# Split of the routed experts' tables in a decoder layer: halves shared by two engines, or whole tables, one engine each

## The chip, the cores and the metric

The kernel runs on one core of one Trainium2 chip. The metric is the device time of one execution in microseconds (us), the median of several runs. A core has five engines that work side by side, each from its own queue of instructions in order: TensorE (PE in the profile; its weight loads are shown apart as PEld), VectorE (DVE), ScalarE (ACT), GpSimd (Pool) and SyncE (SP), which here only starts transfers (DMAs). They wait for one another on semaphores.

## The reference, cut to what matters

One decoder layer over x of 4 x 512 rows of 256 numbers: a Mamba block, then a cross attention, then a mixture of experts, with a layer norm after each. Only the last part is touched:

```
shared = sum over i of _ffn(xf, sw1[i], sw2[i], sw3[i])           # 2 shared experts, all 2048 rows
logits = xf @ router_w.T + expert_bias                            # 8 routed experts
rw, sel = top_k(logits, 2);  rw = softmax(rw)                     # each row goes to 2 of the 8
out = sum over e of combine[:, e] * _ffn(xf, w1[e], w2[e], w3[e])
_ffn(x, w1, w2, w3) = (silu(x @ w1.T) * (x @ w3.T)) @ w2.T        # 256 -> 512 -> 256
```

## The kernel before, in words

The function `experts` runs in three stages. First the first shared expert over all rows (`hidden` and `down`, n = 0 to 3), beside which VectorE sorts the rows by expert. Then the routed experts: the rows, 128 at a time, fill 39 slots (`SLOTS`), each slot with rows of one expert (`owner`). Then the second shared expert (n = 4 to 7), while Pool gathers the slots' results back. The change is in the middle stage and at its two borders.

A product in float32 is made of three: the high part of x by the high part of w, the low part of x by the high part of w, and the high part of x by the low part of w. The high part is a copy rounded to the format fp32r, the low part is the number less its high part. All eight experts' tables lie in on-chip memory (`wall`, per expert three tables of 128 partitions x 1024 columns). Table 0 (w1) and table 1 (w3) of a slot's expert are split anew for each slot, into `wh[0]`, `wl[0]`, `wh[1]`, `wl[1]`; these have one buffer each.

What the engines do for slot j, in the order of their queues:

- TensorE, in the loop near L2400: `turn_x(j+1)` (L2271, two transposes that turn the next slot's rows; they wait until the rows have landed), a read of the slot's owner into a register (`value_load`), `hidden_chosen(j)` (L2289: for part 0 and part 1, that is table 0 and 1, six products: two with x high and w high, two with x low and w high, two with x high and w low), `turn_g(j-1)` (L2300, four transposes) and `down_chosen(j-2)` (L2308). The end of part 0 releases `first_used`, the end of part 1 `h_done`.
- ScalarE, `split_parts(j+1)` (L1925): as soon as `first_used` says that slot j has used table 0, it copies slot j+1's table 0 to `wh[0]`; after `h_done`, table 1 to `wh[1]`. Before the change each copy is two instructions of 512 columns, each of which raises `part_high` by 1. Then `activate(j)` (L1885) and `read_g(j-1)` (L1901).
- VectorE: `read_x(j+1)` (L2065, L2067), the gate of slot j-1 (L2045), `read_y(j-3)` (L2073), then `split_low(j+1, i)` for both tables (L2087): columns 0 to 511 of `wl[i]`.
- Pool: `split_low(j+1, i)` for both tables (L1819): columns 512 to 1023 of `wl[i]`. Behind it in its queue stands `fetch_x(j+3)` (L1834), an indirect DMA that gathers the 128 rows of slot j+3 from DRAM. At j = 8 there stands between them `split_down` (L1824, L1826), which splits the third table of the last shared expert.
- SyncE: after `read_y`, it stores slot j-3's result to DRAM (L1785).

In each part TensorE waits at its fifth product (i = 4) for VectorE's half of the low part and at its sixth (i = 5) for Pool's half. At the first dense product after the slots (`hidden(B, 0)`) it waits, at i = 0 of each part, for the high part and both halves of the low part of the last shared expert's tables, which are split the same way as a fortieth slot.

The order of all queues is written out by hand; no planner sets it.

Of the kernel before, what the change touches and what calls it, by code (L numbers as in the profile page):

```python
# [15 lines left out]
F32 = mybir.dt.float32  # L16
F32R = mybir.dt.float32r
BF16 = mybir.dt.bfloat16
ALU = mybir.AluOpType
ACT = mybir.ActivationFunctionType  # L20
# [1596 lines left out]
def experts(nc, router_t, expert_bias, w1_t, w3_t, w2_t, x2, out):  # L1617
    x2_dram = nc.dram_tensor("e_x2_dram", (NTILE * P, DM), F32, kind="Internal").ap()
    y_dram = nc.dram_tensor("e_y_dram", (SLOTS * P, DM), F32, kind="Internal").ap()
    with ExitStack() as ctx:  # L1620
# [170 lines left out]
        @block.gpsimd  # L1791
        def _(pool):
            nc.gpsimd.memset(ident[:], 0.0)
            nc.gpsimd.memset(lower, 1.0)
            nc.gpsimd.memset(ones, 1.0)
            nc.gpsimd.memset(before, 1.0)
            nc.gpsimd.memset(keep, 1.0)
            nc.gpsimd.memset(half[:], -0.5).then_inc(consts_set, 1)
            pool.wait_ge(consts_set, 1)
            nc.gpsimd.affine_select(out=ident[:], in_=ident[:], compare_op=ALU.not_equal, fill=1.0, base=0,  # L1800
                                    pattern=[[-1, P]], channel_multiplier=1)
            nc.gpsimd.affine_select(out=lower, in_=lower, compare_op=ALU.is_gt, fill=0.0, base=0,
                                    pattern=[[1, E], [-1, E]], channel_multiplier=0).then_inc(consts_set, 1)
            for j in range(3):
                pool.wait_ge(w_high, j + 1)
                nc.gpsimd.tensor_tensor(wl[j][:], raw_first[j], wh[j][:].bitcast(F32), ALU.subtract).then_inc(w_split, 1)
            nc.gpsimd.affine_select(out=before, in_=before, compare_op=ALU.is_gt, fill=0.0, base=0,
                                    pattern=[[1, P]], channel_multiplier=-1)
            nc.gpsimd.affine_select(out=by_expert(keep), in_=by_expert(keep), compare_op=ALU.is_gt, fill=0.0, base=0,
                                    pattern=[[0, E], [1, NTILE]], channel_multiplier=0)  # L1810
            nc.gpsimd.iota(token[:], [[P, NTILE]], base=0, channel_multiplier=1, allow_small_or_imprecise_dtypes=True)
            nc.gpsimd.iota(iota[:], [[1, P]], base=0, channel_multiplier=0,
                           allow_small_or_imprecise_dtypes=True).then_inc(consts_set, 1)

            def split_low(s, i):

                pool.wait_ge(part_high, 4 * s + 2 * i + 2)
                full = wall_of(own[s], i, 512, 1024) if s < SLOTS else shared_raw[i][:, 512:1024]
                nc.gpsimd.tensor_tensor(wl[i][:, 512:1024], full, wh[i][:, 512:1024].bitcast(F32),  # L1819
                                        ALU.subtract).then_inc(part_low_pool, 1)  # L1820

            def split_down():
                pool.wait_ge(raw_loaded[2], 16)
                nc.gpsimd.tensor_copy(wh[2][:], unused[:]).then_inc(w_high, 1)  # L1824
                pool.wait_ge(w_high, 4)
                nc.gpsimd.tensor_tensor(wl[2][:], unused[:], wh[2][:].bitcast(F32), ALU.subtract).then_inc(w_split, 1)  # L1826

            pool.wait_ge(index_ready, 1)
            pool.wait_ge(x2_stored, 16 * B)

            def fetch_x(j):
                if j >= XR:
                    pool.wait_ge(x_turned, j - XR + 1)
                nc.gpsimd.indirect_dma_start(x_row[:, j % XR], None, x2_dram,  # L1834
                                             bass.IndirectOffsetOnAxis(index[:, j:j + 1], 0)).then_inc(x_fetched[j % XR], 16)

            own = {}
            for j in range(XR):
                fetch_x(j)
            for j in range(-1, SLOTS + 2):  # L1840
                if j + 1 < SLOTS:
                    own[j + 1] = pool.value_load(owner[0:1, j + 1:j + 2], min_val=0, max_val=E - 1)
                if j < SLOTS:
                    for i in range(2):
                        split_low(j + 1, i)
                if j == 8:
                    split_down()
                if 0 <= j < SLOTS - XR:
                    fetch_x(j + XR)
            for r in range(2):  # L1850
                pool.wait_ge(y_stored[r], 16 * ((SLOTS + 1 - r) // 2))
            for b in range(B):
                if b > 0:
                    pool.wait_ge(y_fetched[b - 1], 16 * TT * TOPK)
                for t in range(b * TT, (b + 1) * TT):
                    for r in range(TOPK):
                        i = r * NTILE + t
                        nc.gpsimd.indirect_dma_start(y_back[:, r, t], None, y_dram,  # L1858
                                                     bass.IndirectOffsetOnAxis(place_u[:, i:i + 1], 0)).then_inc(y_fetched[b], 16)
            for b in range(B):  # L1860
                rows = slice(b * TT, (b + 1) * TT)
                pool.wait_ge(var_ready, b + 1)
                nc.gpsimd.tensor_tensor(rstd[:, rows], mv[:, rows, 1], half[:], ALU.pow).then_inc(rstd_ready, 1)

        @block.scalar
        def _(act):
# [44 lines left out]
            def split_parts(s):  # L1911

                if s < SLOTS:
                    own[s] = act.value_load(owner[0:1, s:s + 1], min_val=0, max_val=E - 1)
                for i in range(2):
                    if s == 0 or i == 1:
                        act.wait_ge(h_done, U0 + s)
                    else:
                        act.wait_ge(first_used, s)
                    if s == SLOTS:  # L1920
                        act.wait_ge(raw_loaded[i], 16)
                    for h in range(2):
                        half_of = slice(512 * h, 512 * (h + 1))
                        full = wall_of(own[s], i, 512 * h, 512 * (h + 1)) if s < SLOTS else shared_raw[i][:, half_of]
                        nc.scalar.activation(wh[i][:, half_of], full, ACT.Copy).then_inc(part_high, 1)  # L1925

            act.wait_ge(owner_ready, 1)
            act.wait_ge(wall_loaded, 16 * 3 * E)
# [26 lines left out]
        def _(dve):  # L1955
# [124 lines left out]
                                                           ALU.mult, ALU.add)  # L2080
                    step(s)

            def split_low(s, i):

                dve.wait_ge(part_high, 4 * s + 2 * i + 1)
                full = wall_of(own[s], i, 0, 512) if s < SLOTS else shared_raw[i][:, 0:512]
                nc.vector.tensor_tensor(wl[i][:, 0:512], full, wh[i][:, 0:512].bitcast(F32),  # L2087
                                        ALU.subtract).then_inc(part_low_dve, 1)

            def take_stats(b):  # L2090
                for t in range(b * TT, (b + 1) * TT):
# [31 lines left out]
            for n in range(B):  # L2123
# [24 lines left out]
                if n == B - 1:  # L2148
                    dve.wait_ge(owner_ready, 1)
                    own[0] = dve.value_load(owner[0:1, 0:1], min_val=0, max_val=E - 1)  # L2150
                    for i in range(2):
                        split_low(0, i)
                add_dense(n)
            for j in range(-1, SLOTS + 1):
                if j + 1 < SLOTS:
                    read_x(j + 1)
                if 0 <= j < SLOTS - 1:
                    own[j + 1] = dve.value_load(owner[0:1, j + 1:j + 2], min_val=0, max_val=E - 1)
                if j >= 1:
                    gate_on(U0 + j - 1)  # L2160
                if j >= 3:
                    read_y(j - 3)
                if 0 <= j < SLOTS:
                    for i in range(2):
                        split_low(j + 1, i)
            for n in range(B, 2 * B):
                for m in range(MT + 1):
                    if m < MT:
# [26 lines left out]
        def _(pe):  # L2195
# [14 lines left out]
            def hidden(n, m):  # L2210
# [3 lines left out]
                for part, (h, l) in enumerate(((w1h, w1l), (w3h, w3l))):  # L2214
                    terms = [(x, y, k) for x, y in ((h, xth), (h, xtl), (l, xth)) for k in range(KD)]
                    for i, (x, y, k) in enumerate(terms):
                        if n == 0 and m == 0 and i == 4:
                            pe.wait_ge(w_split, part + 1)
                        if n == B and m == 0 and i == 0:
                            pe.wait_ge(part_high, 4 * SLOTS + 2 * part + 2)  # L2220
                            pe.wait_ge(part_low_dve, 2 * SLOTS + part + 1)
                            pe.wait_ge(part_low_pool, 2 * SLOTS + part + 1)
                        mm = nc.tensor.matmul(ps_h[:, u % 2, part], x[:, k, m * P:(m + 1) * P],  # L2223
                                              y[:, k, b * S:(b + 1) * S], start=(i == 0), stop=(i == len(terms) - 1))
                mm.then_inc(h_done, 1)
# [51 lines left out]
            def hidden_chosen(j, e):  # L2277
# [2 lines left out]
                pe.wait_ge(x_read, j + 1)  # L2280
                for part in range(2):
                    terms = [(x, w, k) for x, w in ((xh_col, wh[part]), (xl_col, wh[part]), (xh_col, wl[part])) for k in range(KD)]
                    pe.wait_ge(part_high, 4 * j + 2 * part + 2)
                    for i, (x, w, k) in enumerate(terms):
                        if i == 4:
                            pe.wait_ge(part_low_dve, 2 * j + part + 1)
                        if i == 5:
                            pe.wait_ge(part_low_pool, 2 * j + part + 1)
                        mm = nc.tensor.matmul(ps_h[:, u % 2, part], x[:, j % 2, k * P:(k + 1) * P],  # L2289
                                              w[:, k * HID:(k + 1) * HID], start=(i == 0), stop=(i == len(terms) - 1))  # L2290
                    mm.then_inc(h_done if part else first_used, 1)
# [153 lines left out]
```

## Time and profile before

| | us |
|---|---|
| median of 3 runs | 3066.42 |
| lowest and highest | 3062.02, 3070.91 |
| the profiled execution's own time | 3067.53 |
| its span, first to last instruction | 3065.8 |
| middle stage (39 slots), about | 2756 to 2962 of the span |

Mean granted TensorE clock 0.976 of full speed. Busy time: TensorE 2889.7 us, VectorE 2035.9, ScalarE 1627.6, Pool 1541.1. Busy time says how long an engine worked, not whether anyone waited for it; which work sets the end is read from the chain of waits, which follows from the last instruction back to what released it, and from the timeline of one slot. All starts of instructions below are in us from the span's start.

### The profile page before, as it was taken

The numbers are of one execution on the slowest core, as the hardware profiler recorded it, in microseconds if no ns is written. First come the engines' busy times: TensorE is split into PE (matmuls) and PEld (weight loads), VectorE is DVE, ScalarE is ACT, GpSimd is POOL, SyncE is SP. The second block draws the span as 40 slices with busy tenths as digits, with TensorE's granted clock in tenths as the row PEclk, the third lists the DMA queues.
The fourth block names the chain that finished last, engine by engine and source line by source line (L and its number), as shares of the span: only waits on it lengthen the run. The fifth ranks groups of instructions, "written<-read, shape, count | busy, mean of one in ns | idle before, by whom it ended". The sixth has DMA issues, their size and how long they took to land. (4 is left out here: it accounts for less than half of the span.)

```text
span 3065.8 us, 36316 instructions
## 1 busy us (share of the span) xinstructions
PE 2889.7 (94%) x12038; PEld 1914.8 (62%) x12038; DVE 2035.9 (66%) x3484; ACT 1627.6 (53%) x2816; POOL 1541.1 (50%) x1198
## 2 busy tenths in 40 slices
PE   7577999999999999999999999999999999889996
PEld 3234565656665656565656565656777776677886
DVE  5897777775658677656677766565555555456656
ACT  5753445453445454535454544356777778425651
POOL 4495667671017575600276755003666657307753
PEclk9798999999999999999999999999999999799998
DMA  6352312111122121211221212010111100511112
GB/s 236 148 177 90 90 38 59 35 52 57 39 70 59 35 66 32 69 36 39 76 60 36 59 36 79 23 41 13 46 39 22 39 15 15 172 68 42 53 51 69
DMA packets 71694, 189.98 MB, mean 62 GB/s; under 512 B 8420, under 2 KB 39272, under 8 KB 63448
## 3 DMA queue, kind: packets, MB, share of 16 engines
q1 hardware_dynamic: 67096, 172.08, 18.5%
q0 software_dynamic: 3984, 15.60, 1.6%
q8 instruction: 98, 1.61, 0.2%
q14 instruction: 84, 0.69, 0.1%
q10 hardware_dynamic: 432, 0.01, 0.0%
HBM read 124.59 MB, written 28.44 MB: 50 GB/s over the span
## 5 line engine op out<-in xcount | busy, mean ns | idle before, releaser
L1131 ACT ACTIVATE a_carry<-a_st 128x512 f32<-128x512 f32 (+1 forms) x1088 | 648.6, 596 | 920.7 <-PE a_st L1567 907.7
L1587 PE MATMUL a_o<-a_carry,a_vals 128*65 128x512 f32 (+1 forms) x1632 | 836.7, 594 | 0.0
L1316 DVE TENSOR_REDUCE a_maxes<-a_mx 128x1 f32<-128x512 f32 x1016 | 677.4, 686 | 191.7 <-PE a_mx L1490 184.6
L949 POOL TENSOR_TENSOR a_plow<-a_carry,a_phigh 128x512 fp32r<-128x512 f32 (+1 forms) x272 | 348.6, 1288 | 260.0 <-ACT a_phigh L1134 256.3
L979 POOL TENSOR_TENSOR a_shared<-a_shared,a_bc 128x512 f32<-128x512 f32 x192 | 250.4, 1304 | 388.6 <-DVE a_shared L1251 388.6
L1567 PE MATMUL a_st<-a_q,a_kone 65*128 65x512 f32 (+1 forms) x1088 | 431.7, 397 | 0.0
L1251 DVE TENSOR_TENSOR_SCAN a_shared<-a_shared 128x512 f32<-128x512 f32 x192 | 290.6, 1515 | 15.5 <-POOL a_shared L968 14.2
L1566 PE MATMUL a_st<-a_q,a_keven 128*128 128x512 f32 (+1 forms) x544 | 296.6, 545 | 1.3 <-ACT a_q L1108 0.9
L1566 PE MATMUL a_st<-a_q,a_kodd 128*128 128x512 f32 (+1 forms) x544 | 286.9, 527 | 0.0
L1490 PE MATMUL a_mx<-a_kodd,a_q 128*128 128x512 f32 x512 | 276.1, 555 | 10.2 <-DVE a_maxes L1316 8.6
L1567 PEld LDWEIGHTS a_st<-a_q,a_kone 65*128 65x128 f32 (+1 forms) x1088 | 202.1, 186 | 124.0 <-issue 93.5
L1490 PE MATMUL a_mx<-a_keven,a_q 128*128 128x512 f32 x504 | 252.5, 545 | 14.7 <-DVE a_maxes L1316 10.4
L983 POOL TENSOR_TENSOR a_y<-a_y,a_shared 128x512 f32<-128x512 f32 x192 | 257.1, 1339 | 15.2
L1587 PEld LDWEIGHTS a_o<-a_carry,a_vals 128*65 128x65 f32 (+1 forms) x1632 | 212.9, 137 | 75.1 <-issue 0.2
L1429 PE MATMUL a_ring<-a_kvh,a_wt 128*128 128x512 f32 (+2 forms) x776 | 231.2, 379 | 8.6 <-DVE a_kodd L1295 3.4
L968 POOL TENSOR_TENSOR a_shared<-a_carry,a_bc 128x512 f32<-128x512 f32 x96 | 145.7, 1519 | 160.0 <-DMA a_bc<-m_kept_bc 160.0
L1490 PEld LDWEIGHTS a_mx<-a_keven,a_q 128*128 128x128 f32 x504 | 95.5, 190 | 145.5 <-DVE a_maxes L1316 61.6
L1429 PE MATMUL a_ring<-a_wt,a_kvh 128*128 128x256 f32 (+1 forms) x1088 | 177.3, 285 | 0.0
L1134 ACT ACTIVATE a_phigh<-a_carry 128x512 fp32r<-128x512 f32 (+1 forms) x272 | 172.0, 632 | 8.7
L1429 PEld LDWEIGHTS a_ring<-a_kvh,a_wt 128*128 128x128 f32 x776 | 143.4, 192 | 49.4 <-DVE a_q L1289 14.0
L1429 PEld LDWEIGHTS a_ring<-a_wt,a_kvh 128*128 128x128 f32 (+1 forms) x1088 | 159.4, 187 | 17.9 <-issue 3.3
L1566 PEld LDWEIGHTS a_st<-a_q,a_keven 128*128 128x128 f32 (+1 forms) x544 | 101.4, 186 | 110.2 <-issue 71.9
(292 smaller groups left out, 5228.8 us busy)
## 6 DMA issues: line engine op xcount, KB each, us to landing
a_bc<-m_kept_bc SPq DMA_DIRECT2D x48, 512.0 KB, 3.7
a_wt<-a_w_split SPq DMA_DIRECT2D x15, 1536.0 KB, 9.6
a_kone<-a_keven SPq DMA_DIRECT2D x32, 528.5 KB, 4.5
a_kone<-a_kodd SPq DMA_DIRECT2D x32, 528.5 KB, 4.2
e_wall<-in_w_t_dram SPq DMA_DIRECT2D x27, 512.0 KB, 5.4
a_shared<-m_kept_bc SPq DMA_DIRECT2D x16, 512.0 KB, 3.8
a_w_split<-a_wt POOLq DMA_DIRECT2D x4, 1536.0 KB, 5.5
a_shared<-in_ctx_dram SPq DMA_DIRECT2D x4, 1536.0 KB
```

The lines of the kernel that those rows point to most:

```text
L949: nc.gpsimd.tensor_tensor(p_low(s)[0:r], p_of(s % 4)[0:r], p_high(s)[0:r].bitcast(F32), ALU.subtract).then_inc(p_low_ready, 1)
L979: nc.gpsimd.tensor_tensor(state[:, u % 2], state[:, u % 2], bc[:, i % 2, 1], ALU.mult).then_inc(seen_ready, 1)
L983: nc.gpsimd.tensor_tensor(y[:, c], y[:, c], state[:, u % 2], ALU.add).then_inc(y_added, 1)
L1131: nc.scalar.activation(p_of(s % 4)[0:r], st[0:r, s % 2], ACT.Exp, scale=SCALE).then_inc(exp_done, 1)
L1134: nc.scalar.activation(p_high(s)[0:r], p_of(s % 4)[0:r], ACT.Copy).then_inc(p_high_ready, 1)
L1251: nc.vector.tensor_tensor_scan(state_of(b, u), dA, dB, 0.0, ALU.mult, ALU.add).then_inc(scanned, 1)
L1316: nc.vector.reduce_max(maxes[:, c, t:t + 1], mx_bank(g, i), AX_X).then_inc(mx_max, 1)
L1429: mm = nc.tensor.matmul(out, x(k), y(k), start=(j == 0), stop=(j == len(terms) - 1))
L1490: mm = nc.tensor.matmul(mx_bank(g, i), qd[of(g)][:, t * P:(t + 1) * P], kk[:, c * 512:(c + 1) * 512], start=True, stop=True)
L1566: nc.tensor.matmul(st[0:r, s % 2], keys_of(g)[:, kt * P:kt * P + r], qd[of(g)], start=True, stop=False)
L1567: nc.tensor.matmul(st[0:r, s % 2], k_one[g % 2][0:DH + 1, kt * P:kt * P + r], qm[of(g)][0:DH + 1, :], start=False, stop=True).then_inc(st_ ...
L1587: nc.tensor.matmul(ps_o[0:DH + 1, g % 2], vals[0:r, kt * HG + j, :], p_of(s % 4)[0:r], start=(kt == 0), stop=(kt == KT - 1)).then_inc(pv_d ...
```

## The change

ScalarE copies each table in one instruction of 1024 columns instead of two of 512, and raises `part_high` once per table. VectorE makes the whole low part of table 0 (1024 columns), Pool the whole low part of table 1. TensorE waits, at the fifth product of part 0, for VectorE alone, and at the fifth product of part 1 for Pool alone. The counts of the semaphores follow. The core of the diff:

```diff
@@ Pool
-            def split_low(s, i):
-                pool.wait_ge(part_high, 4 * s + 2 * i + 2)
-                full = wall_of(own[s], i, 512, 1024) if s < SLOTS else shared_raw[i][:, 512:1024]
-                nc.gpsimd.tensor_tensor(wl[i][:, 512:1024], full, wh[i][:, 512:1024].bitcast(F32),
-                                        ALU.subtract).then_inc(part_low_pool, 1)
+            def split_low(s):
+                pool.wait_ge(part_high, 2 * s + 2)
+                full = wall_of(own[s], 1, 0, 1024) if s < SLOTS else shared_raw[1]
+                nc.gpsimd.tensor_tensor(wl[1][:], full, wh[1][:].bitcast(F32), ALU.subtract).then_inc(part_low_pool, 1)
...
@@ ScalarE, split_parts
-                    for h in range(2):
-                        half_of = slice(512 * h, 512 * (h + 1))
-                        full = wall_of(own[s], i, 512 * h, 512 * (h + 1)) if s < SLOTS else shared_raw[i][:, half_of]
-                        nc.scalar.activation(wh[i][:, half_of], full, ACT.Copy).then_inc(part_high, 1)
+                    full = wall_of(own[s], i, 0, 1024) if s < SLOTS else shared_raw[i][:, 0:1024]
+                    nc.scalar.activation(wh[i][:], full, ACT.Copy).then_inc(part_high, 1)
@@ VectorE
-            def split_low(s, i):
-                dve.wait_ge(part_high, 4 * s + 2 * i + 1)
-                full = wall_of(own[s], i, 0, 512) if s < SLOTS else shared_raw[i][:, 0:512]
-                nc.vector.tensor_tensor(wl[i][:, 0:512], full, wh[i][:, 0:512].bitcast(F32),
-                                        ALU.subtract).then_inc(part_low_dve, 1)
+            def split_low(s):
+                dve.wait_ge(part_high, 2 * s + 1)
+                full = wall_of(own[s], 0, 0, 1024) if s < SLOTS else shared_raw[0][:, 0:1024]
+                nc.vector.tensor_tensor(wl[0][:], full, wh[0][:].bitcast(F32), ALU.subtract).then_inc(part_low_dve, 1)
@@ TensorE, hidden (first dense product after the slots)
-                            pe.wait_ge(part_high, 4 * SLOTS + 2 * part + 2)
-                            pe.wait_ge(part_low_dve, 2 * SLOTS + part + 1)
-                            pe.wait_ge(part_low_pool, 2 * SLOTS + part + 1)
+                            pe.wait_ge(part_high, 2 * SLOTS + part + 1)
+                            pe.wait_ge(part_low_pool if part else part_low_dve, SLOTS + 1)
@@ TensorE, hidden_chosen
-                    pe.wait_ge(part_high, 4 * j + 2 * part + 2)
+                    pe.wait_ge(part_high, 2 * j + part + 1)
                     for i, (x, w, k) in enumerate(terms):
                         if i == 4:
-                            pe.wait_ge(part_low_dve, 2 * j + part + 1)
-                        if i == 5:
-                            pe.wait_ge(part_low_pool, 2 * j + part + 1)
+                            pe.wait_ge(part_low_pool if part else part_low_dve, j + 1)
```

The three places that call `split_low` for i = 0 and 1 call it once.

## Rows read from the trace of the kernel before

**Rows 1.** The page, busy time of each engine over the span.
```profile
PE 2889.7 (94%) x12038; PEld 1914.8 (62%) x12038; DVE 2035.9 (66%) x3484; ACT 1627.6 (53%) x2816; POOL 1541.1 (50%) x1198
```
**Rows 2.** Busy time by window: length, engines with counts, granted clock, DMA share, GB/s.
```profile
2840.00:2900.00 60.00, 60.00 (x303) 50.37 (x302) 41.66 (x71) 37.96 (x70) 44.34 (x36) 1.00 0.17 54
```
**Rows 3.** Chain of waits, middle stage (start, length, what); a timeline row stands between.
```profile
2847.34 0.44 PE e_o L2300 x4
...
2852.47 0.44 PE e_o L2300 x4
...
2857.82 0.44 PE e_o L2300 x4
...
2935.19 0.44 PE e_o L2300 x4
...
2942.50 0.23 PEld L2271 LDWEIGHTS e_o<-e_ident,e_x_row 128*128 128x128 f32 x2
...
2943.25 3.00 PE e_h L2289 x12
2946.25 0.44 PE e_o L2300 x4
```
**Rows 4.** Timeline of two slots: start, length, engine, line, idle before in brackets.
```profile
2852.59 1.15 ACT L1925 ACTIVATE e_wh<-e_wall 128x512 fp32r x2 [0.21 <-PE e_h L2289]
...
2855.68 0.97 POOL L1834 DMA_INDIRECT e_x_row<-e_x_dram,e_index  x1 [0.15 <-issue]
...
2856.56 1.15 ACT L1925 ACTIVATE e_wh<-e_wall 128x512 fp32r x2 [1.85 <-PE e_h L2289]
...
2857.34 0.69 DVE L2087 TENSOR_TENSOR e_wl<-e_wall,e_wh 128x512 fp32r<-128x512 f32 x1 [0.26 <-ACT e_wh L1925]
...
2857.91 2.97 POOL L1819 TENSOR_TENSOR e_wl<-e_wall,e_wh 128x512 fp32r<-128x512 f32 x2 [1.25 <-ACT e_wh L1925]
...
2858.72 1.01 DVE L2087 TENSOR_TENSOR e_wl<-e_wall,e_wh 128x512 fp32r<-128x512 f32 x1 [0.69 <-ACT e_wh L1925]
...
2862.10 0.41 PEld L2289 LDWEIGHTS e_h<-e_wl,e_xh_col 128*128 128x128 f32 x2
```
**Rows 5.** Groups of instructions with 1024 columns elsewhere: busy us, mean ns.
```profile
L1869 ACT ACTIVATE e_wh<-e_wall 128x1024 fp32r<-128x1024 f32 x3 | 3.2, 1057 | 15.4 <-DMA e_wall<-in_w_t_dram 15.4
...
L1806 POOL TENSOR_TENSOR e_wl<-e_wall,e_wh 128x1024 fp32r<-128x1024 f32 x3 | 7.0, 2351 | 4.8 <-ACT e_wh L1869 4.8
...
L1972 DVE TENSOR_TENSOR e_gate<-e_raw 128x1024 f32<-128x1024 f32 x1 | 1.2, 1225 | 0.0
```
**Rows 6.** Landings: gathers, 2772 to 2962; the store at 2939.8; all stores; one store's start.
```profile
DMA to landing us min/median/max: 2.7/2.8/4.0
...
DMA to landing us min/median/max: 3.0/3.0/3.0
...
e_y_dram<-e_y_row SPq DMA_DIRECT2D x37, 128.0 KB, 1.9
...
L1785 SPq DMA_DIRECT2D e_y_dram<-e_y_row x1: 320/320/320, 2857.1 to 2857.1; - x1
```
**Rows 7.** Start of the middle stage: one timeline row, then three of the chain.
```profile
2749.94 2.19 ACT L1925 ACTIVATE e_wh<-e_wall 128x512 fp32r x4 [0.30 <-issue]
...
2752.11 1.03 DVE e_wl L2087
...
2756.76 4.59 PE e_h L2289 x12
...
2764.23 2.79 DMA e_x_row<-e_x_dram,e_index
```
**Rows 8.** Chain of waits at the slot where Pool also runs `split_down`.
```profile
2809.64 3.04 DMA e_x_row<-e_x_dram,e_index
```
**Rows 9.** Timeline at the border to the last stage.
```profile
2962.03 1.15 ACT L1925 ACTIVATE e_wh<-e_equal 128x512 fp32r<-128x512 f32 x2 [0.24 <-PE e_h L2289]
...
2965.16 0.41 PEld L2223 LDWEIGHTS e_h<-e_xth,e_wh 128*128 128x128 f32 x2
```

More of the change, by code:

```diff
@@ L1843, in _ @@
                 if j < SLOTS:
-                    for i in range(2):
-                        split_low(j + 1, i)
+                    split_low(j + 1)
                 if j == 8:
@@ L2150, in _ @@
                     own[0] = dve.value_load(owner[0:1, 0:1], min_val=0, max_val=E - 1)
-                    for i in range(2):
-                        split_low(0, i)
+                    split_low(0)
                 add_dense(n)
@@ L2163, in _ @@
                 if 0 <= j < SLOTS:
-                    for i in range(2):
-                        split_low(j + 1, i)
+                    split_low(j + 1)
             for n in range(B, 2 * B):
```

## The prediction

> **What bounds the kernel now.** I read the page first: TensorE is busy 94% of the span and every other engine at most 66% [rows 1]. Then busy time by window, since the change touches only the 39 slots between about 2756 and 2962: there TensorE is busy 60.00 of 60.00 us at full clock, VectorE 41.66, ScalarE 37.96, Pool 44.34 [rows 2]. So in the stage the shorter work of VectorE or ScalarE is worth nothing by itself; what counts is whether something TensorE waits for comes later. Third, the chain of waits. Call E(j) the end of slot j's hidden products, which is where its four transposes start; two ordinary ones are 2847.34 and 2852.47, 5.13 us apart, all of it TensorE's own work [rows 3]. The next is 2857.82, 5.35 later: not ordinary. The last view, the timeline of those slots [rows 4], says which loop nearly binds beside TensorE.
>
> **The loop through Pool's gather.** Pool's queue holds the low parts and, behind them, the gather of rows for slot j+3. Pool starts it at 2855.68, which is 3.21 after E = 2852.47; in other ordinary slots it is 3.22 [rows 3, 4]. The gather lands L later, ordinarily 2.8 [rows 6]. TensorE's transposes of those rows wait for it, and in its queue stand behind them the register load and the hidden products. Where the landing is late: gather at 2938.41, landed 4.0 later at 2942.41 [rows 6], transposes loaded at 2942.50, products at 2943.25, end at 2946.25, so 0.75 from the transposes to the products and 3.00 for the products [rows 3]. With a wake-up of 0.05 that is
>
> E(j+2) = the later of E(j+1) + 5.13 and E(j) + D + L + 3.81, with D = 3.22 now.
>
> For the slot just named: 2935.19 + 3.22 + 4.0 + 3.81 = 2946.22, measured 2946.25. I ran this rule over all 37 ends from 2772.20 to 2961.99 with the 34 landings of the trace (24 of them 2.7 to 3.0, ten of 3.3 to 4.0); no end is off by more than 0.2. The gather becomes late when L exceeds 10.26 - 7.03 = 3.23: an ordinary landing has 0.43 us to spare per two slots, and the ten long ones already cost.
>
> **The change, part by part.** (a) ScalarE's copies: two of 512 columns take 1.15 [rows 4], one of 1024 takes 1.06 [rows 5]. But each consumer now waits for the whole table. (b) VectorE: two instructions a slot of 0.69 and 1.01 [rows 4] become one of 1.22 [rows 5]. It starts when table 0's copy ends, 2856.56 + 1.06 + 0.2 = 2857.8, and ends at 2859.0. TensorE wants it at the fifth product of part 0 of the next slot, which is about 1.4 before the load at 2862.10 [rows 4], so at 2860.7: 1.7 to spare, cost nothing. If that cover were gone it would need to be 1.7 late first. (c) Pool: now it can start at table 0's copy, 2857.91, and ends both halves at 2860.88, E + 3.06 [rows 4]. After, it can't start before table 1's copy is whole: E + 0.12 (2852.59 against 2852.47 [rows 3, 4]) + 1.06 + 0.20 (copy's end 2857.71 to Pool's start 2857.91) + 2.35 for 1024 columns [rows 5] = E + 3.73. So Pool, though it works 0.62 less per slot, ends 0.67 later. (d) Its low part is due at the fifth product of part 1, load at 2862.10 = E + 4.28 [rows 3, 4]; with a wake-up of 0.06 there is 0.49 to spare. Cost nothing; if Pool's instruction took as long as now its pair does (2.97), it would be 0.13 late each slot. (e) Queued behind it on Pool is the gather: D becomes 3.22 + 0.67 = 3.89. For an ordinary landing the loop takes 3.89 + 2.8 + 3.81 = 10.50 per two slots against TensorE's 10.26: 0.24 late in two slots. This is the term that I think decides. TensorE's part 0 no longer waits for Pool, but it did not wait before either.
>
> **The sum.** Two such loops interleave (even and odd slots), so what one loses gives the other slack: each landing counts half. The 23 ordinary ones cost 0.12 each, 2.8; the ten long ones 0.67/2 each, 3.3; the slot in which Pool also splits the third table, whose gather at 2809.64 ends a wait now [rows 8], moves by 0.66. The rule run slot by slot with D = 3.89 gives +6.7 in all, where every landing stays as it is.
>
> It may not. The store of a finished slot is issued at 2857.1, 1.4 after the gather at 2855.68 [rows 4, 6], and tied to the next slot's E, not to Pool. After, the gather is issued 0.67 later against it, so both 128 KB transfers are under way together. No row shows that overlap cleanly. From below: an ordinary landing stays 2.8 (0); a shorter one nothing suggests. From above: 1.2, the excess of the longest landing, 4.0 over 2.8, beside which the store landed after 3.0 instead of 1.9 [rows 6]. I take 0.15, near the lower end, because the ordinary landings of the trace, with the store close behind, all lie within 2.7 to 2.9; that is 33 x 0.15/2 = 2.5. At the upper end it would be 20.
>
> The Trainium skill ("DMA: Bandwidth & Descriptors", Queues, rings and completion order) says that each DMA engine goes round-robin between the queues that have work, a packet at a time. By that rule two equal transfers that start together both end late, and this term lies above zero; it gives no figure that I use.
>
> Start of the stage: ScalarE's first copy starts at 2749.94, so VectorE's whole low part ends at 2749.94 + 1.06 + 0.17 + 1.22 = 2752.4 instead of 2753.14 [rows 7], and the additions and transposes behind it come 0.7 sooner. Hidden products of slot 0 end at 2761.35 - 0.7 = 2760.65 [rows 7]; table 1's copy + 1.17, Pool + 0.20 + 2.35, gather + 0.15: 2764.5, against 2764.23 [rows 7]. On its heels VectorE's next low part may hold up the gather; the pair at 2809.64 took 3.04 instead of 2.79 [rows 7, 8]. So +0.3 to +0.6, I take 0.4. End of the stage: table 1 of the last shared expert is copied from 2962.03; Pool ends at 2962.03 + 1.06 + 0.20 + 2.35 = 2965.64, and TensorE now loads for that part at 2965.16 [rows 9], waiting at the first product, not the fifth. Late by 0.5; I take 0.5. What follows hangs on TensorE and moves with it.
>
> Together 6.7 + 2.5 + 0.4 + 0.5 = +10.1 us. On the profiled execution's 3067.53 that is 3077.6; this execution is 1.1 above the median of 3066.42, so I predict 3076.5.
>
> **Lock between VectorE and Pool.** VectorE's half takes 1.01 when Pool is in the middle of its pair and 0.69 alone [rows 4]; it ends 0.54 after Pool's first instruction would. After, VectorE's instruction (E to E + 1.2) ends before Pool's starts (E + 1.4), so both lose the delay, which is why I use 1.22 and 2.35. The Trainium skill ("SBUF — State Buffer", SBUF: two separate sides) calls the pair of ports that the two share an exclusive lock, held for a whole instruction. The trace agrees with it here (1.01 against 0.69); by it the change is a relief for both engines, 0.3 us each per slot, but not for TensorE.
>
> **Rivals.**
> 1. *The gather's loop has more slack than my rule says* (the 0.75 is the price of a register load after a long idle, and would hide behind running products when the delay is 0.1 to 0.2). For it: the smallest delay that the trace shows is for landings of 3.4, nothing between. Against: 37 ends follow one rule. Then only long landings, the middle slot and the borders pay: 0 to 2 + 0.7 + 0.4 + 0.5, about +2.5: 3069. This is the case that ends not slower.
> 2. *Collision.* VectorE's 1.22 is 0.2 short of Pool's start and 0.3 behind the gather's end; when VectorE starts while Pool holds the ports it waits the whole 2.35, or holds up the gather by the 0.25 seen [rows 7, 8], or store and gather share the DMA engines fully. One such 0.3 to 0.6 on every L: 5 to 10 more, +15 to +20, 3084; the upper end of 1.2 would give +28. For it: the margins; against: both are released by TensorE, so their order repeats.
> 3. *Faster.* The 0.7 gained at the start keeps TensorE's clock up: slot 0's twelve products take 4.59 [rows 7] where a late but full-speed slot takes 3.00 [rows 3], so up to 1.6, perhaps twice, and the gather's loop is slack. Gain 2 or so, 3064: within measurement. More than that no row supports.
>
> **How the numbers follow.** Forecast 0.60, rival 1 0.22, rival 2 0.13, rival 3 0.05. 0.3% of the time is 9.2 us, about what a measurement of this kernel can tell from no change. The forecast's own range is +6.5 to +15 (3073 to 3082), a little over half of it above 9.2; with rival 2 slower has 0.33 + 0.13 = 0.46. Faster by more than 9 has nothing but chance: 0.04. Within: 0.50. The range of 8 in 10 reaches to rival 1 below and to rival 2's nearer half above: 3067 to 3086.
>
> **What would show it.** Right: E to E about 5.2 to 5.3 instead of 5.13 in ordinary slots, with TensorE idle before its hidden products ("issue") or before the transposes of x (released by the gather) in most slots; the gather 3.9 after E; Pool's instruction 2.35, VectorE's 1.22. Wrong: TensorE busy 60 of 60 in the same window (rival 1); Pool's mean above 2.6 or VectorE's above 1.4 (rival 2); waits of TensorE for Pool's low part in ordinary slots, which would contradict (d).

## The result, and the profile after

| | before | after |
|---|---|---|
| median of 5 runs, us | 3067.78 | 3081.55 |
| lowest and highest | 3062.02, 3070.91 | 3079.78, 3084.34 |
| profiled execution: own time, span | 3067.53, 3065.8 | 3079.78, 3077.6 |

The ratio of the times is 1.0047, 95% interval 1.0032 to 1.0062: slower by 13.8 us, with 10.1 forecast; the median of 3081.55 lies between the forecast of 3076.5 and the upper end of the range, 3086. (Of the 5.05 us above 3076.5, 1.4 is the median before, 3067.78 over five executions instead of the 3066.42 that the forecast started from.) The same kernel run again later gave 3078.76 beside 3065.01, 1.0046 (1.0032 to 1.0059). By the profiled executions the span grew by 11.8, and that is the sum accounted for below.

The page's engine line, which answers to [rows 1]:

```profile
PE 2895.8 (94%) x12038; PEld 1915.8 (62%) x12038; DVE 2012.4 (65%) x3444; ACT 1622.4 (53%) x2736; POOL 1528.4 (50%) x1158
```

VectorE has 23.5 us less work, ScalarE 5.2, Pool 12.7, and the kernel is slower. TensorE's busy time grew by 6.1. The two windows, of the ordinary slots ([rows 2] before) and of the slot with `split_down` (columns: length, PE, PEld, VectorE, ScalarE, Pool, granted clock, DMA share, GB/s):

```profile
2840.00:2900.00 60.00, 58.51 (x290) 48.10 (x289) 34.13 (x56) 34.10 (x45) 36.90 (x23) 1.00 0.18 49
2806.00:2823.00 17.00, 13.11 (x59) 10.52 (x58) 8.73 (x12) 6.29 (x9) 11.83 (x7) 0.90 0.10 31
```

TensorE is idle for 1.49 of the 60 us where it was idle for none, and in the 17 us around the slow slot for 3.89, where it was 2.79 at a granted clock of 1.00. The chain of waits shows two ordinary gaps (start, length, what; [rows 3] before):

```profile
2852.37 0.44 PE e_o L2290 x4
...
2857.53 0.44 PE e_o L2290 x4
...
2859.91 0.35 issue
2860.26 2.98 PE e_h L2279 x12
2863.24 0.44 PE e_o L2290 x4
...
2868.36 0.44 PE e_o L2290 x4
```

From E to E it is 5.16, 5.71, 5.12. Every other slot has a short stop of TensorE before the hidden products; the chain calls it "issue". I read it as the register load that stands in TensorE's queue between the late transposes and the hidden products; the profile names no releaser for it. The timeline of these slots says who is late (start, length, engine, line; idle before in brackets; [rows 4] before):

```profile
2856.30 0.97 POOL L1833 DMA_INDIRECT e_x_row<-e_x_dram,e_index  x1 [0.16 <-issue]
...
2857.49 1.22 DVE L2083 TENSOR_TENSOR e_wl<-e_wall,e_wh 128x1024 fp32r<-128x1024 f32 x1 [0.50 <-ACT e_wh L1921]
2857.65 1.06 ACT L1921 ACTIVATE e_wh<-e_wall 128x1024 fp32r x1 [0.31 <-PE e_h L2279]
...
2858.90 2.38 POOL L1819 TENSOR_TENSOR e_wl<-e_wall,e_wh 128x1024 fp32r<-128x1024 f32 x1 [1.64 <-ACT e_wh L1921]
...
2860.23 0.30 PEld L2279 LDWEIGHTS e_h<-e_wh,e_xh_col 128*128 128x128 f32 x2 [0.56 <-issue]
...
2861.42 0.97 POOL L1833 DMA_INDIRECT e_x_row<-e_x_dram,e_index  x1
```

The gathers start at 2856.30 and 2861.42, which is 3.93 after E = 2852.37 and 3.89 after E = 2857.53; before it was 3.21. The waits of the whole stage, 2760 to 2970 (who waited, for whom: us in total, times, longest):

```profile
PEld e_o L2263 <- DMA e_x_row<-e_x_dram,e_index: 10.5, 10, 4.0
PEld e_h L2279 <- issue: 8.9, 19, 0.6
```

Before, these rows had 4.8 in 2 waits and 2.5 in 7. The landings of the 33 gathers and of the stores, 2777 to 2970, then the gathers alone:

```profile
e_y_dram<-e_y_row SPq DMA_DIRECT2D x34, 128.0 KB, 2.6
e_x_row<-e_x_dram,e_index POOLq DMA_INDIRECT x33, 3.1
...
DMA to landing us min/median/max: 2.9/3.1/4.1
```

They were 1.9 and 2.8 [rows 6]. (In this trace a landing is recorded for 22 of the 33 gathers; in the second trace of the same kernel, e0 below, for all, and the median is 3.1 there too.)

Two places depart from the pattern. The slot with `split_down` ([rows 8] before), in the timeline and then in the chain:

```profile
2808.77 2.36 POOL L1825 TENSOR_TENSOR e_wl<-e_unused,e_wh 128x1024 fp32r<-128x1024 f32 x1
...
2809.04 3.18 DVE L2083 TENSOR_TENSOR e_wl<-e_wall,e_wh 128x1024 fp32r<-128x1024 f32 x1 [0.48 <-ACT e_wh L1921]
...
2811.29 1.79 POOL L1833 DMA_INDIRECT e_x_row<-e_x_dram,e_index  x1
```

```profile
2811.29 3.51 DMA e_x_row<-e_x_dram,e_index
...
2815.59 4.37 PE e_h L2279 x12
```

TensorE's wait there, on the timeline of after and then of before:

```profile
2814.84 0.46 PE L2263 MATMUL e_o<-e_ident,e_x_row 128*128 128x128 f32 x2 [3.60 <-DMA e_x_row<-e_x_dram,e_index]
```

```profile
2812.72 0.44 PE L2271 MATMUL e_o<-e_ident,e_x_row 128*128 128x128 f32 x2 [2.48 <-DMA e_x_row<-e_x_dram,e_index]
```

And the start of the stage, in the chain ([rows 7] before):

```profile
2749.08 1.07 ACT e_wh L1921
...
2755.13 2.99 PE e_h L2279 x12
...
2762.01 3.60 DMA e_x_row<-e_x_dram,e_index
...
2766.51 4.97 PE e_h L2279 x12
2771.48 0.44 PE e_o L2290 x4
```

**Where the 11.8 us went**, from the starts of the four transposes of all 39 slots (from the first to the last of them 201.99 before and 215.82 after; the first comes 2.3 sooner after, so this grows by more than the span):

| part | predicted | measured |
|---|---|---|
| everything ahead of the stage (ScalarE's first copy at 2749.08, was 2749.94) | 0 | -0.9 |
| start of the stage, to the third E | +0.4 | +0.2 |
| slot with `split_down` (gap 8.39 before, 10.88 after) | +0.7 | +2.5 |
| the other slots (mean gap 5.18 to 5.45) | +8.5 | +9.4 |
| last slot and border | +0.5 | +0.4, and 0.2 behind it |
| sum | +10.1 | +11.8 |

The predicted column splits the 6.7 and the 2.5 of the prediction: 0.7 of the 6.7 was the slot with `split_down`.

### The profile page after: what moved, and what is told of

Read it like the earlier page. It is cut to its first block and busy times, and to the rows that moved or that the text cites. A ratio compares the mean times of both kernels' runs of the same rounds, so it can differ in the third digit from the quotient of the medians.

```text
span 3077.6 us, 35999 instructions
## 1 busy us (share of the span) xinstructions
PE 2895.8 (94%) x12038; PEld 1915.8 (62%) x12038; DVE 2012.4 (65%) x3444; ACT 1622.4 (53%) x2736; POOL 1528.4 (50%) x1158
```

## The experiments

All of them were timed beside the kernel before on the same chip. Theory G is the prediction's: what costs is the delay D from E to Pool's gather, plus a longer landing. The rivals differ by kernel and stand in the expectations.

**1. Gather moved ahead of the low parts.** In Pool's loop body `fetch_x(j+3)` goes to the top, so it stands behind `split_low(j)` instead of `split_low(j+1)`: one slot, 5.13 us, sooner. Once in the kernel after (e1), once in the kernel before (e2); e0 is the kernel after again.

```diff
             for j in range(-1, SLOTS + 2):
+                if 0 <= j < SLOTS - XR:
+                    fetch_x(j + XR)
                 if j + 1 < SLOTS:
                     own[j + 1] = pool.value_load(...)
...
                 if j == 8:
                     split_down()
-                if 0 <= j < SLOTS - XR:
-                    fetch_x(j + XR)
```

> The changed kernel once more, as the measure for the others of this group on one chip. Both theories: about 13.8 us above the kernel before, as measured (3081.6 against 3067.8).

> The changed kernel, with one move on Pool: the gather of slot j+3 is issued ahead of slot j+1's low part instead of behind it, so it goes out one slot (5.13 us) earlier. Theory (the gather's loop, E(j+2) = E(j) + D + L + 3.81, is what costs): the loop no longer binds, TensorE is busy all the time in ordinary slots, E to E 5.13; left are a wait of about 1.3 for Pool's low part in slot 1, about 1.2 behind the split of the third table, 0.4 at the last border. 13.8 + 3.4 + 2 us less than the changed kernel: 3062, range 3058 to 3066, below the kernel before. Rival (Pool's low part, or ScalarE's whole copies, are themselves late in ordinary slots): nothing or little changes, 3078 to 3082.

> The kernel before, with the same move on Pool alone. Theory: its ten long landings and the waits at slots 3 and 11 for the gather go, less a new wait of about 1.2 for Pool's low part behind the split of the third table: 4 to 5 us less, 3063, range 3060 to 3066. Rival (the gather has slack enough before the change): no change, 3067. Against the run with the changed split it also tells what that split is worth once the gather is out of the way: by the theory within 2 us of it.

| | us | before | ratio (95%) |
|---|---|---|---|
| e0, after again | 3078.76 | 3065.01 | 1.0046 (1.0032 to 1.0059) |
| e1, after with gather first | 3059.48 | 3065.01 | 0.9992 (0.9972 to 1.0012) |
| e2, before with gather first | 3060.53 | 3065.01 | 0.9987 (0.9978 to 0.9996) |

One of e1's eleven executions took 3091.52 and widens its interval. The window of ordinary slots in e1:

```profile
2840.00:2900.00 60.00, 60.00 (x307) 50.67 (x306) 36.31 (x60) 35.55 (x47) 39.71 (x24) 1.00 0.18 49
```

With the whole change in place and only the gather sooner, TensorE is busy 60.00 of 60.00, no wait on the gather is left, and 19.3 us go. What is left of waits for Pool's low part are two at the start of the stage (1.36 and 1.30) and one beside `split_down` (2.02), where the gap is 7.18. Landings in e1 are still 3.1 (gather) and 2.6 (store), and they cost nothing. So the loop through the gather is the whole loss, and a longer landing counts only inside that loop. Rival 1 of the prediction (slack in the loop) falls with e0, which repeats the loss, and whole-table splits cost nothing of their own in the ordinary slots, where e1's gaps are 5.13.

**2. The delay alone, without the change.** In the kernel before, Pool fills three tables that nothing reads any more between its low parts and the gather (0.31 + 0.20 + 0.20 us).

```diff
                 if 0 <= j < SLOTS - XR:
+                    if j > 0:
+                        pool.wait_ge(padded, 3 * j)
+                    for t in (hot[:]..., iota[:], chosen[:]...):
+                        nc.gpsimd.memset(t, 0.0).then_inc(padded, 1)
                     fetch_x(j + XR)
```

> The kernel before, its split untouched; on Pool three fills of tables that nobody reads any more stand between a slot's low parts and the gather (0.7 to 0.8 us together, from 0.2 us for each 128 columns of a fill). Theory (only the lateness of the gather matters): D goes from 3.22 to about 3.95 as in the changed kernel, with everything else as before: slower by what the stage of the changed kernel lost, +8 to +12: 3073 to 3078, E to E alternating between 5.13 and 5.5 or more, ordinary landings 3.1. Rival (the loss comes from whole tables, late low parts or ScalarE's longer copies): time as before, 3065.

Measured 3073.83 beside 3064.04, ratio 1.0027 (1.0017 to 1.0038): +9.8. One slot's fills and gather on Pool's timeline:

```profile
2855.94 0.31 POOL L1853 MEMSET e_hot<- 128x256 f32 x1
2856.19 0.20 POOL L1853 MEMSET e_iota<- 128x128 f32 x1
2856.33 0.20 POOL L1853 MEMSET e_chosen<- 128x128 f32 x1
2856.69 0.97 POOL L1835 DMA_INDIRECT e_x_row<-e_x_dram,e_index  x1 [0.16 <-issue]
```

and its landings over the stage:

```profile
e_y_dram<-e_y_row SPq DMA_DIRECT2D x36, 128.0 KB, 2.5
e_x_row<-e_x_dram,e_index POOLq DMA_INDIRECT x33, 3.0
```

The gather starts 3.76 after the chain's E = 2852.93, 0.55 later than before. That alone, with every table split as before, brings the pattern of the changed kernel back: gaps of 5.13 and 5.4 in turn, landings of 3.0 and 2.5. The longer landing thus comes from the gather's later place against the store, not from the new instructions. The +9.8 is not all of this kind, though: by the trace the 35 gaps between the start and the last slot, the one with `split_down` left out, sum to 5.2 more than before (9.4 in the changed kernel), and 2.1 are lost at the start of the stage.

**3. The store kept out of the gather's way.** In the kernel after, SyncE waits with the store of slot j until the gather for slot j+5 has landed.

```diff
                 sp.wait_ge(y_read, j + 1)
+                if j + 5 < SLOTS:
+                    sp.wait_ge(x_fetched[(j + 5) % XR], 16 * ((j + 5) // XR + 1))
                 sp.dma_start(y_dram[j * P:(j + 1) * P], y_row[:, j % 2])...
```

> The changed kernel; SyncE stores a slot's result only when the gather that is under way has landed, so that the two transfers don't overlap. Theory (an ordinary landing is 3.1 instead of 2.8 in the changed kernel because the store now runs beside the gather): ordinary landings go back to 2.8, and 33 landings x 0.3 / 2 = 4 to 5 us are saved: 3077, range 3075 to 3079. Rival (the landings are longer for another reason, such as Pool's issue): landings stay at 3.1, time 3081 to 3082.

Measured 3076.17 beside 3065.01, 1.0038 (1.0025 to 1.0052): 2.6 below e0. The landings:

```profile
e_y_dram<-e_y_row SPq DMA_DIRECT2D x36, 128.0 KB, 1.7
e_x_row<-e_x_dram,e_index POOLq DMA_INDIRECT x33, 2.8
```

Both fall back (the gather from 3.1, the store from 2.6, with a landing recorded for 19 of the 39 stores), and the ordinary long gap shrinks from about 5.57 to 5.2 to 5.4. The overlap of the two transfers is therefore what made the landing longer. Its price is 2.6 by the medians, less than the 4 to 5 expected here (3.1 by the 35 gaps of the two traces, 189.7 us in e0 and 186.6 in e4); the intervals of e0 and e4 overlap, so the landings show the overlap more surely than the time does.

**4. One part of the change alone.** The kernel before with ScalarE's whole copies only (and the counts that their consumers wait for); VectorE and Pool still share each table.

```diff
-                    for h in range(2):
-                        half_of = slice(512 * h, 512 * (h + 1))
-                        ...
-                        nc.scalar.activation(wh[i][:, half_of], full, ACT.Copy).then_inc(part_high, 1)
+                    full = wall_of(own[s], i, 0, 1024) if s < SLOTS else shared_raw[i][:, 0:1024]
+                    nc.scalar.activation(wh[i][:], full, ACT.Copy).then_inc(part_high, 1)
```

> The kernel before with only ScalarE's part of the change: one copy of 1024 columns per table; VectorE and Pool still make a half of each low part. They now become free at the same moment and meet at the ports that they share. Theory: what counts is when Pool is done: its pair grows by up to one VectorE half more (0.3 to 0.5), D 3.3 to 3.6, +1 to +4 us: 3066 to 3069. Rival (the whole copy itself is what costs, since consumers wait longer for it): most of the 13.8 us, 3075 or more.

Measured 3069.37 beside 3064.04, 1.0012 (1.0003 to 1.0021): +5.3, where +1 to +4 was expected. Pool's timeline:

```profile
2852.05 3.48 POOL L1819 TENSOR_TENSOR e_wl<-e_wall,e_wh 128x512 fp32r<-128x512 f32 x2 [0.56 <-ACT e_wh L1923]
...
2855.69 0.97 POOL L1834 DMA_INDIRECT e_x_row<-e_x_dram,e_index  x1 [0.16 <-issue]
```

The chain's E is 2852.04, so D is 3.65: both engines are now released by the same copy, meet, and Pool's pair takes 3.48 instead of 2.97. A part of the loss comes with the whole copies, by the same route. The slot with `split_down` took 10.30 instead of 8.39, with a granted clock of 0.90 around it; that is 1.9 of the 5.3, and the expectation had no such term. The kernels with one slot order stand in a row (mean gap: of the 35 ordinary slots, as in the table of the result):

| kernel | D, us | median landing, gather and store | mean gap | time above before, us |
|---|---|---|---|---|
| before | 3.21 | 2.8, 1.9 | 5.18 | 0 |
| e6, whole copies | 3.65 | 2.9, 2.3 | 5.27 | +5.3 |
| e3, fills | 3.76 | 3.0, 2.5 | 5.33 | +9.8 |
| e4, after, store later | 3.90 | 2.8, 1.7 | 5.33 | +11.2 |
| after (e0) | 3.90 | 3.1, 2.6 | 5.42 | +13.8 |

**5. The tables swapped.** In the kernel after, Pool takes table 0, which is copied 1.4 us sooner, and VectorE table 1.

```diff
@@ Pool
-                pool.wait_ge(part_high, 2 * s + 2)
-                full = wall_of(own[s], 1, 0, 1024) if s < SLOTS else shared_raw[1]
-                nc.gpsimd.tensor_tensor(wl[1][:], full, wh[1][:].bitcast(F32), ...)
+                pool.wait_ge(part_high, 2 * s + 1)
+                full = wall_of(own[s], 0, 0, 1024) if s < SLOTS else shared_raw[0][:, 0:1024]
+                nc.gpsimd.tensor_tensor(wl[0][:], full, wh[0][:].bitcast(F32), ...)
@@ VectorE the other way round; TensorE's waits follow
```

> The changed kernel with the two tables exchanged: Pool makes the low part of table 0 (whose copy is ready 1.4 us earlier), VectorE that of table 1. Theory: Pool ends at E + 2.4 and the gather is issued at E + 2.6 instead of 3.9, but VectorE, kept from the shared ports until E + 2.4, then holds them to E + 3.5 and the gather's issue with them (L about 3.6); D + L is 6.2, below the 6.45 at which the loop binds. In its place VectorE is late: gate at E + 4.7 to 5.4 where TensorE's transposes of it want it by about E + 5.1, 0.2 us per slot. Together 3068 to 3074, under the changed kernel, with TensorE waiting for the gate and not for the gather. Rival (the order on Pool doesn't matter, the whole tables as such cost): as the changed kernel, 3078 to 3081.

Measured 3073.95 beside 3063.88, 1.0034 (1.0022 to 1.0047). The timeline of one slot:

```profile
2859.95 2.37 POOL L1819 TENSOR_TENSOR e_wl<-e_wall,e_wh 128x1024 fp32r<-128x1024 f32 x1 [0.88 <-ACT e_wh L1921]
...
2861.28 2.12 DVE L2083 TENSOR_TENSOR e_wl<-e_wall,e_wh 128x1024 fp32r<-128x1024 f32 x1 [0.94 <-ACT e_wh L1921]
...
2862.46 1.78 POOL L1833 DMA_INDIRECT e_x_row<-e_x_dram,e_index  x1
```

VectorE starts beside Pool's instruction and takes 2.12 instead of 1.22; it ends at 2863.40, and Pool's gather, issued at 2862.46, takes 1.78 instead of 0.97. The gather's median landing over the stage is 3.6:

```profile
e_y_dram<-e_y_row SPq DMA_DIRECT2D x35, 128.0 KB, 1.7
e_x_row<-e_x_dram,e_index POOLq DMA_INDIRECT x33, 3.6
```

The gather is issued 2.5 after E, and D + L, about 6.1, is below the 6.45 (10.26 less 3.81) at which the loop binds. TensorE's waits, 2760 to 2970, show who is late instead:

```profile
PEld e_o L2290 <- DVE e_gate L2041: 11.0, 18, 1.5
PEld e_o L2263 <- DMA e_x_row<-e_x_dram,e_index: 2.3, 1, 2.3
```

The gather's loop no longer binds; the gates do, which VectorE computes late because its low part starts later and takes 2.12. The gaps are 5.43 and 5.34 in turn. So the gain is lost in the collision of the two engines, as expected, but through VectorE's queue and not through the gather: rival 2 of the prediction in a milder form. The time, 10.1 above its kernel before, is more than the 0.2 to 6.2 that 3068 to 3074 meant above 3067.8, and by the time alone the other reading in the expectation (3078 to 3081) is as near; the waits tell them apart. In the kernel after the collision happens only in two places, at the start and beside `split_down`.

**6. `split_down` moved to the end** (`if j == SLOTS:` for `if j == 8:`), alone in the kernel after (e9), and with the gather first in the kernel after (e7) and before (e8).

> The changed kernel with split_down moved from slot 8 to the end of the slots, the gather left behind the low part. Theory: the slot of 10.89 us (a late gather, its issue held up by VectorE's low part, and a TensorE at half clock behind the wait) becomes an ordinary one of 5.2 to 5.5; the alternation of 5.13 and 5.6 in the others stays: 5.4 us less than the changed kernel, 3073, range 3072 to 3075. It shares out the 13.8 us: about 5 of the changed kernel's excess over a kernel without such a slot sit there (3 of them were in the kernel before too).

> The changed split with the gather issued first, and the split of the third table (split_down) moved from slot 8 to the end of the slots on Pool. Theory: the slot of 7.19 us in the trace of the gather-first kernel becomes 5.13, nothing else changes: 2.1 us less, 3057 to 3058; Pool has some 10 us free between its last low part and the gathers of the results. Rival (the third table is then late for the last stage, or Pool's first gather of results): 3059 or more.

> The split of before with the gather first and split_down last. Theory: the slots of 6.05, 5.52, 5.35 and 5.22 us behind split_down become 5.13: 1.6 us less than with the gather first alone, 3059. Against the same with whole tables it tells what the change itself is worth once nothing else is late: within 1.5 us either way (0.4 against it at the last border, up to 1 for it at the start).

| | us | before | ratio (95%) |
|---|---|---|---|
| e9, after | 3073.55 | 3063.88 | 1.0035 (1.0022 to 1.0047) |
| e7, after, gather first | 3057.82 | 3064.04 | 0.9975 (0.9964 to 0.9985) |
| e8, before, gather first | 3057.77 | 3064.04 | 0.9978 (0.9969 to 0.9987) |

The window of that slot in e9:

```profile
2806.00:2823.00 17.00, 16.33 (x83) 13.30 (x82) 9.56 (x16) 9.36 (x13) 10.01 (x6) 1.00 0.20 50
```

The gap falls from 10.9 to 5.7 and the granted clock there goes from 0.90 back to 1.00. e9 stands 9.7 above its kernel before, e0 13.8 above its own: 4.1 less, with 5.4 expected. This is not all a loss of the change: the kernel before spends 8.39 in that slot and so keeps some 3 us that e9 has got rid of. e7 and e8 beat both kernels, the one before by 6 us, and do not differ from one another (0.05 us): with the gather out of Pool's way the change is worth nothing in either direction that these medians show. In e7 all gaps between the first and the last two are 5.13. Against e1 and e2, each beside its own kernel before, the move of `split_down` is worth 0.7 in e7, where 2.1 was expected (the gap does fall from 7.18 to 5.13), and 1.8 in e8, where it was 1.6.

## Why the prediction was right

**What bounds.** Right. TensorE's own 5.13 with the gather's loop just under it; e1 and e3 show it from both sides.

**(c), (e): Pool's low part and D.** Right to 0.04 us: Pool's instruction 2.38 against 2.35, gather 3.89 and 3.93 after E against 3.89. The rule holds slot by slot: gather at 2877.87, landed after 3.5, gives 2885.18, and E is 2885.18. In e0, with all landings recorded, it gives 34 of the 35 ends within 0.13; the one that it misses, by 1.4, is the slot with `split_down`, where TensorE's clock fell.

**The 6.7 and the landing's 2.5.** Right in sum for the ordinary slots (9.4 against 8.5), and partly by luck, since the two terms missed in opposite directions. e4 has the delay without the longer landings: 35 x (5.33 - 5.18) = 5.2 for the delay, where 6.0 was forecast. The rest is the longer landing, 35 x (5.42 - 5.33) = 3.1 by e0 and 4.2 by the first trace (mean gap 5.45), where 2.5 was forecast: the median landing grew by 0.3, not 0.15. I also expected all gaps at 5.2 to 5.3; they are 5.13 and about 5.57 in turn, 5.35 in the mean. One of the two interleaved loops carries the whole delay and the other runs free, which the prediction's halving had allowed for in the sum but not in the picture. Experiment 3 shows that the longer landing comes from the overlap with the store.

The Trainium skill ("DMA: Bandwidth & Descriptors", Queues, rings and completion order) has each DMA engine go round-robin between the queues that have work. By that rule both of two overlapping transfers end later. The trace agrees: 2.8 to 3.1 and 1.9 to 2.6.

**The slot with `split_down`, 0.7 of the 6.7.** The term that was mis-sized: 2.5 measured. Of it, 0.64 is the later gather (2.20 after TensorE's last E at 2809.09), as forecast. 0.47 is a longer landing, 3.51 against 3.04: VectorE's instruction, now 1024 columns, takes 3.18 beside Pool's, and the gather's issue behind it takes 1.79 (it was 1.25). And 1.37 is TensorE at a lower clock, twelve products in 4.37 instead of 3.00, in a window of mean granted clock 0.90, after a wait of 3.60; before, a wait of 2.48 there left the clock at 1.00. The second trace of this kernel, e0, repeats all three: gather 2.21 after E, landing 3.59, products in 4.45 after a wait of 3.68. That the longer wait is what brought the clock down is likely but not shown: e6 and e5 lost it in this slot after waits of 2.80 and 1.94, and e3 kept it after 2.72. I had seen both mechanisms, the hold-up at the start [rows 7, 8] and the clock in the 4.59 of slot 0, and priced neither for this slot. e9 takes the whole slot's loss away, the older part included.

**Start, 0.4.** Near in sum, not in its parts. Slot 0 ran at full clock (2.99 against 4.59), which was rival 3's mechanism, but slot 1 waited 0.54 for VectorE's low part and 1.33 for Pool's, the gather was held up as feared (issue 1.77, landing 3.60), and slot 2's products took 4.97. Slot 2 was below full clock before too, so the gain of slot 0 went to the waits of slot 1 and to a somewhat slower slot 2.

**(b), (d): no waits for the low parts in ordinary slots.** Right; in the stage TensorE waited for Pool's once and for VectorE's once, both at its start.

**End, 0.5.** Right: the last gap is 5.33 instead of 4.92.

**Rivals.** 1 fell with the windows and e3. 2, the collision, is real, but only in two places, as its counter-argument said; e5 shows a collision in every slot, and there it costs about 0.2 us a slot through VectorE's gates. 3 happened in slot 0 and was eaten.

**Open.** Why some of the landings take 3.3 to 4.1 in both kernels was not tried. What brought the clock down in the middle slot was not tried by itself. The 2 us between the medians (13.8) and the profiled executions (11.8) are within the spread of the runs.

## What to carry to other kernels

Before work is given to an engine, look at what stands behind it in that engine's queue: here Pool worked less per slot and the kernel was slower, because its single instruction started later and a gather stood behind it. A transfer whose inputs are ready should be issued ahead of elementwise work that waits for others; that one move took away the whole loss and some 5 us more. And when TensorE reads 60 of 60 us busy, compute the slack of the loops beside it: 0.43 us per two slots was all there was.

## What the runs showed of the hardware that I had not expected

- A VectorE instruction with two SBUF inputs holds up the issue of an indirect DMA on Pool: 0.97 becomes 1.77 to 1.79 (start, middle slot, 33 of the 36 gathers of e5 from 2760 on), and the issue ends 0.84 to 0.86 after VectorE's instruction in each of them. In all of these VectorE's was under way when the issue began; two issues of e5 that began within 0.01 us of it took 0.97 and 0.98. The landing takes 3.5 to 3.6 at these two places and by e5's median, instead of 2.8.
- VectorE's 1024-column subtraction takes 1.22 alone, 2.12 where it meets Pool's in e5, 3.18 beside Pool's `split_down`.
- A 128 KB gather and a 128 KB store under way together cost each other: 2.8 to 3.1 and 1.9 to 2.6, and back to 2.8 and 1.7 when the store waits.
- TensorE's clock after a wait: 2.48 us idle left the next twelve products at 3.0 (granted clock 1.00, the 2.4 GHz level); 3.60 idle in the middle slot gave 4.37; at the start of the stage 2.57 idle, with 0.90 idle shortly before it, gave 4.97. So the fall costs 1.4 to 2 us where it comes, on top of the wait. The length of the last wait doesn't tell whether it comes: in the same slot 2.72 idle left 2.99 in e3, and 1.94 idle gave 4.58 in e5.
